# Edge counting in 196 steps, 14 buffered rows, 3125 sources per pass, and one unit's scores made a phase earlier

## The reference

```
x = x + gat8(layernorm(x))       # 8 heads of 32 channels, softmax over each node's incoming edges
x = x + moe(layernorm(x))        # 16 experts, top 2
x = x + gat_3_layers(normalised) # 3 single-head attention layers, 256 channels, gelu between them
x = x + routed_ffn(layernorm(x)) # top half of the tokens through an FFN
```

## Time and profile before

| | us |
|---|---|
| median of three runs | 3741.9 (3736.48 to 3748.98) |
| the profiled execution | 3744.81 |
| its span | 3743.1 |
| edges and nodes (phase 1) | 0 to 66.9 |
| edge counting (phase 2) | 66.9 to 458.1 |
| heads (phase 3) | 458.1 to 1856.5 |
| experts and projection | 1856.5 to 2402 |
| three layers and the last FFN | 2402 to 3743 |

### The profile page before, as it was taken

How to read it: one execution, slowest core, us unless ns; L and a number is a source line. 1 busy time by engine, 2 the same in 40 slices (tenths; PEclk the granted TensorE clock), 3 DMA queues, 4 the chain that set the end, 5 groups by cost and what they waited for, 6 DMA issues and landing times. The chain is left out here.

```text
span 3743.1 us, 70138 instructions
## 1 busy us (share of the span) xinstructions
PE 3425.8 (92%) x27405; PEld 2680.2 (72%) x27406; DVE 2828.5 (76%) x4285; ACT 2523.6 (67%) x4088; POOL 300.4 (8%) x279
## 2 busy tenths in 40 slices
PE   6999889989999898998668999699999999999999
PEld 4565566666666666666458999588878888788777
DVE  7999999999999999999662222665556555676594
ACT  5899899999999999999710111366656665676532
POOL 1000010000000000000003444000000000000000
PEclk9999999999999999999859999899999999999999
DMA  5433211112114121111268885323323232423101
GB/s 163 155 109 140 99 55 65 64 55 73 55 63 202 55 73 55 62 67 55 66 202 267 238 237 150 128 104 106 113 76 119 106 114 75 173 104 121 38 22 35
DMA packets 146630, 398.54 MB, mean 106 GB/s; under 512 B 20163, under 2 KB 92252, under 8 KB 128252
## 3 DMA queue, kind: packets, MB, share of 16 engines
q1 hardware_dynamic: 127542, 354.64, 26.8%
q0 software_dynamic: 15552, 36.16, 4.1%
q10 hardware_dynamic: 3206, 3.20, 0.3%
HBM read 331.96 MB, written 61.99 MB: 105 GB/s over the span
## 5 line engine op out<-in xcount | busy, mean ns | idle before, releaser
L994 PE MATMUL hd_psT<-ident,hd_scores 128*128 128x128 f32 (+1 forms) x5000 | 721.6, 282 | 13.6 <-ACT hd_scores L896 13.6
L905 ACT ACTIVATE hd_probsT<-hd_psT 128x768 f32<-128x768 f32 (+1 forms) x800 | 658.9, 850 | 69.0 <-PE hd_psT L994 69.0
L959 DVE SCALAR_TENSOR_TENSOR hd_scores<-el_heads,hx 128x3136 f32<-128x3136 f32 x200 | 694.9, 3475 | 0.0
L1008 PE MATMUL hd_psO<-hd_probsT,hx 128*32 128x128 f32 (+1 forms) x10000 | 571.3, 281 | 135.1 <-ACT hd_probsT L905 135.1
L963 DVE CUSTOM_DVE_ANT_0 hd_scores<-hd_scores,mask_heads 128x3136 f32<-128x3136 f32 x200 | 684.1, 3421 | 8.6
L896 ACT ACTIVATE hd_scores<-hd_scores,hd_negmax 128x1664 f32<-128x1664 f32 (+1 forms) x400 | 647.9, 1620 | 18.8 <-DVE hd_negmax L963 18.8
L994 PEld LDWEIGHTS hd_psT<-ident,hd_scores 128*128 128x128 f32 (+1 forms) x5000 | 531.8, 140 | 162.7 <-issue 162.7
L1526 PE MATMUL ly_psO<-hx_a,ly_probsT 128*128 128x256 f32 x2500 | 584.0, 381 | 0.0
L1008 PEld LDWEIGHTS hd_psO<-hd_probsT,hx 128*32 128x32 f32 (+1 forms) x10000 | 316.9, 108 | 332.3 <-ACT hd_probsT L905 225.7
L1475 ACT ACTIVATE ly_probsT<-ly_psT 128x768 f32<-128x768 f32 (+1 forms) x300 | 248.4, 828 | 391.8 <-PE ly_psT L1515 391.6
L1526 PEld LDWEIGHTS ly_psO<-hx_a,ly_probsT 128*128 128x128 f32 x2500 | 453.9, 189 | 71.4 <-issue 16.6
(11 more groups left out here) (337 smaller groups left out, 3957.3 us busy)
## 6 DMA issues: line engine op xcount, KB each, us to landing
ly_mask<-mask_dram SPq DMA_DIRECT2D x75, 1568.0 KB, 6.6
mask_heads<-mask_dram SPq DMA_DIRECT2D x48, 1568.0 KB, 6.6
moe_w<-in_L_ffn_w SPq DMA_DIRECT2D x144, 512.0 KB
mask_dram<-logc SPq DMA_DIRECT2D x200, 196.0 KB, 1.9
el_heads<-el_dram POOLq DMA_DIRECT2D x4, 1568.0 KB, 19.3
el_heads<-el_slope_dram POOLq DMA_DIRECT2D x4, 1568.0 KB, 23.0
el_heads<-el_dram SPq DMA_DIRECT2D x4, 1568.0 KB, 10.1
el_heads<-el_slope_dram SPq DMA_DIRECT2D x4, 1568.0 KB, 14.2
```

The lines of the kernel that those rows point to most:

```text
L905: nc.scalar.activation(pT[:, gi % 2, 0:w], psT[gi % 2][:, 0:w], ACT.Copy).then_inc(s_ev, 1)
L959: nc.vector.scalar_tensor_tensor(sc[:, c, :], el[:, h, 0, :], hx[:, b, o:o + 1], el[:, h, 1, :], ALU.subtract, ALU.min).then_inc(s_lk, 1)
L994: last = nc.tensor.transpose(psT[gi % 2][0:r, t * P:(t + 1) * P], sc[:, u % 3, c0:c0 + r], g["ident"][:, :])
L1008: last = nc.tensor.matmul(psO[B % 3][cg * CH:(cg + 1) * CH, h * P:(h + 1) * P], hx[0:r, tt, c0:c0 + CH], pT[0:r, gi % 2, t * P:(t + 1) * P ...
```

## The change

The diff cut to what it does; every use of a score tile in `heads_phase` and `layers_phase` changes from NS to N columns in the same way as those shown.

```diff
-WIN = NP // DL
+WIN = -(-N // DL)
-RUN = 40
+RUN = 28
+LASTROWS = WIN * DL - (NB - 1) * P
...
-def adjacency_phase(nc, g, el, mask):
+def adjacency_phase(nc, g, hx, el, mask, sc_first, nm):
-        SS, AHEAD, ROWS, LATE, OUT = 4, 3, 10, 2, 4
+        SS, AHEAD, ROWS, LATE, OUT = 4, 3, 14, 2, 4
...
-        logc = sb("logc", [P, ROWS, SC])
+        logc = el[:, HG - 1, :, :].rearrange("p i n -> p (i n)")[:, 0:ROWS * SC].rearrange("p (r c) -> p r c", c=SC)
...
             blocks(dve, windows)
+            dve.wait_ge(s_el, 16 * 2 * (HG - 1))
+            dve.wait_ge(s_first, 32)
+            nc.vector.scalar_tensor_tensor(sc_first[:, :], el[:, 0, 0, 0:N], hx[:, 0, D:D + 1], el[:, 0, 1, 0:N],
+                                           ALU.subtract, ALU.min).then_inc(s_lk, 1)
+            dve.wait_ge(s_lk, 1)
+            nc.vector.memset(spare[:, :], 0.0)
+            nc.vector.tensor_tensor_reduce(out=sc_first[:, :], in0=sc_first[:, :], in1=mask[:, 0, 0:N], scale=1.0,
+                                           scalar=3.0e38, op0=ALU.add, op1=ALU.min, accum_out=nm[:, 0:1]).then_inc(s_nm, 1)
+            dve.wait_ge(s_nm, 1)
...
-            for h in range(HG):
+            for h in range(HG - 1):
                 for i, rows in enumerate((g["el_dram"], g["el_slope_dram"])):
                     pool.dma_start(el[:, h, i, :], rows[h:h + 1, 0:NS].broadcast_to([P, NS])).then_inc(s_el, 16)
...
-        sc = sb("scores", [P, 3, NS])
+        sc = [sc_first] + [sb(f"scores{i}", [P, N]) for i in range(1, 3)]
...
         @block.sync
         def _(sp):
+            load_el(sp, 0, HG - 1, 0)
+            load_el(sp, 0, HG - 1, 1)
             for B in range(2, BLOCKS):
...
-                sp.dma_start(mask[:, B % 2, :], g["mask_dram"][b * P:(b + 1) * P, :]).then_inc(s_mask[B % 2], 16)
+                r = P if b < NB - 1 else LASTROWS
+                sp.dma_start(mask[0:r, B % 2, :], g["mask_dram"][b * P:b * P + r, :]).then_inc(s_mask[B % 2], 16)
...
-                if b == 0 and q:
-                    dve.wait_ge(s_el[h], 32 * q)
+                if b == 0 and (q or h == HG - 1):
+                    dve.wait_ge(s_el[h], 32 * (q + (h == HG - 1)))
...
-                nc.vector.scalar_tensor_tensor(sc[:, c, :], el[:, h, 0, :], hx[:, b, o:o + 1], el[:, h, 1, :],
+                nc.vector.scalar_tensor_tensor(sc[c][:, :], el[:, h, 0, 0:N], hx[:, b, o:o + 1], el[:, h, 1, 0:N],
...
-            maxima(0)
+            dve.sem_inc(s_lk, 1)
+            dve.sem_inc(s_nm, 1)
             maxima(1)
...
-        sc = sb("scores", [P, 3, NS])
+        sc = sb("scores", [P, 3, N])
```

More of the change, by code:

```diff
@@ L23 @@
 assert NS >= N and DL * SA == P
-WIN = NP // DL
+WIN = -(-N // DL)
 WPB = P // DL
-RUN = 40
-assert WIN % RUN == 0
+RUN = 28
+assert WIN % RUN == 0 and WIN % 2 == 0
+LASTROWS = WIN * DL - (NB - 1) * P
 ET = -(-E // P)
@@ L85, in edges_nodes_phase @@
         ei = sb("edge_int", [P, 2, EC, P], I32)
-        srcT = sb("srcT", [P, ECOL])
-        dstT = sb("dstT", [P, ECOL])
+        srcT, dstT = (sc_first[:, n:n + ECOL] for n in (0, ECOL))
         tmm = sb("tile_minmax", [P, 2, EC])
@@ L118, in edges_nodes_phase @@
         xT = sb("p0_xT", [P, 2, 2, P])
-        wn = sb("p0_wn", [P, 2, D])
-        wT = sb("p0_wT", [P, 2, D])
+        wn, wT = (sc_first[:, n:n + 2 * D].rearrange("p (k d) -> p k d", k=2) for n in (2 * ECOL, 2 * ECOL + 2 * D))
         A = sb("p0_A", [P, 2, 2 * HEADS])
@@ L801, with heads_phase @@
 CUT = T0[2] * P
-assert sum(TG) * P >= NS > (sum(TG) - 1) * P
+assert sum(TG) * P >= N > (sum(TG) - 1) * P
 @phase
-def heads_phase(nc, g, hx, el, mask, y_dram):
+def heads_phase(nc, g, hx, el, mask, sc_first, nm, y_dram):
     with ExitStack() as ctx:
@@ L962, in maxima @@
                 nc.vector.memset(spare[:, :], 0.0)
-                nc.vector.tensor_tensor_reduce(out=sc[:, c, :], in0=sc[:, c, :], in1=mask[:, B % 2, :],
+                nc.vector.tensor_tensor_reduce(out=sc[c][:, :], in0=sc[c][:, :], in1=mask[:, B % 2, 0:N],
                                                scale=1.0, scalar=3.0e38, op0=ALU.add, op1=ALU.min,
@@ L992, in transposes @@
                     c0 = (T0[gi] + t) * P
-                    r = min(P, NS - c0)
-                    last = nc.tensor.transpose(psT[gi % 2][0:r, t * P:(t + 1) * P], sc[:, u % 3, c0:c0 + r], g["ident"][:, :])
+                    r = min(P, N - c0)
+                    last = nc.tensor.transpose(psT[gi % 2][0:r, t * P:(t + 1) * P], sc[u % 3][:, c0:c0 + r], g["ident"][:, :])
                 last.then_inc(s_T, 1)
@@ L1291, in maxima @@
                 nc.vector.memset(spare[:, :], 0.0)
-                nc.vector.tensor_tensor_reduce(out=sc[:, c, :], in0=sc[:, c, :], in1=mask[:, B % 2, :],
+                nc.vector.tensor_tensor_reduce(out=sc[:, c, :], in0=sc[:, c, :], in1=mask[:, B % 2, 0:N],
                                                scale=1.0, scalar=3.0e38, op0=ALU.add, op1=ALU.min,
@@ L1300, in first_maxima @@
                 c = B % 3
-                cols = (slice(0, EARLY * P), slice(EARLY * P, NS))[part]
+                cols = (slice(0, EARLY * P), slice(EARLY * P, N))[part]
                 if part == 0:
@@ L2186, in program @@
             mask = sbh("mask_heads", [P, 2, NS])
+            sc_first = sbh("scores0", [P, N])
+            nm = sbh("negmax", [P, 3])
             with ExitStack() as early:
```

28 lines of the change are left out of this document (15 added, 13 removed).

## The result

The changed kernel takes 3724.0 us (median of 6 runs, 3716.37 to 3730.57); the kernel before, on the same chip, 3742.2 (6 runs). The ratio is 0.9948, with a 95% interval of 0.9928 to 0.9968: faster by 12 to 27 us, 18.2 by the medians. A second comparison (4 runs against 14) gave 3724.0 against 3739.0: 14.9 us by the medians, ratio 0.9954 (0.9940 to 0.9969). The forecast was 3719.3, between 3710 and 3732, and faster.

A forecast was written before the change was run, and what follows sets the result against it. VectorE was taken to bound the counting and heads phases, TensorE the layers. The terms 7.4 + 5.2 + 5.4 + 4.6 = 22.6 us off the median 3741.9 gave 3719.3 us, range 3710 to 3732.

The forecast's parts named there:

- The bounds: VectorE bounds counting and heads phase, so its savings there come off the end; TensorE bounds the layers, where they don't.
- Four steps: Edge counting: four steps fewer at VectorE's period of 1.857 us save 7.4 us.
- The ring and the loads: Early counting: fourteen rows for ten and six early loads for eight remove ScalarE's waits for stores, saving 5.2 us.
- Unit 0: Crossing from counting to heads: unit 0's score passes fill VectorE's idle time, saving 6.87 less J, 5.4 us.
- J: Cost of VectorE's branch over the looped steps, ahead of unit 0's passes: 0 to 3.3 us, taken as 1.5.
- 3125 columns: Heads phase: eleven columns fewer a pass save 22.9 ns a unit, 4.6 us over 199 units; nothing in the layers.
- The fourth head: Start of heads phase: its late-loaded scores land at 12.3 us, needed at 14.0, so no wait; at worst 1.8 us.
- The crooked buffers: Rival, layers: score buffers off 64-byte boundaries slow TensorE's weight loads, total 3755 to 3897 us; chance 0.05.
- Late loads: Rival, start of heads phase: late fourth head's loads or a long branch, total 3722.9 or 3724.7 us; chance 0.22.
- a ring whose wait moves: Rival, counting: fourteen rows only put the store wait four steps later, total 3724.5 us; chance 0.07.
- ScalarE as the limit: Rival, heads phase: ScalarE becomes the limit and up to 4.6 us of the columns go, 3723.9 us; chance 0.03.

The follow-up runs named there:

- the run without the late clock: The changed kernel with 200 steps for 196, run a second time: counting 387.6 us, total 3723.2 us.
- the reverse experiment: The changed kernel with 3136 columns for 3125 in the heads phase's passes and unit 0's: heads 1391.7 us, total 3727.6 us, ratio 0.9961.

## Why the prediction was right

**The bounds.** VectorE bounds the counting and the heads phase: four steps more, a wait before unit 3, eleven columns more and unit 0 put back each came out at the end of their phase, within 0.5 us of their price once the low clocks are taken off. The layers didn't move with the columns.

**Four steps, 7.4.** Measured 7.8 in the run without the late clock, 7.2 without the 0.6 us at the diagonal.

**The ring and the loads, 5.2.** All of it came: VectorE's steps lost 5.2 us at the waits before, and nothing after. The reason given, slack against the longest landing, held with eight loads too, but its count was wrong. A row is stored nearly three steps after its logarithm and not two, so ten rows leave 13.1 us for 14.9, and fourteen 20.5 for 22.3. The term came out all the same, since 20.5 is over every landing measured (19.5 at most). The same count is why ring 10 with six loads was expected to have no wait, and had one.

**Unit 0, 5.4.** Measured 5.7. The term that was off is J, taken as 1.5 and bounded by 0 and 3.3; it was 1.08. TensorE's row was the right neighbour for the bound and too far for the value. The passes then ended 1.0 us after the last store had landed (447.1 and 446.1), which is what the branch costs, as the step said. The Trainium skill's rule (Runtime: NRT & Kernel Launch, instruction fetch mechanics), that a taken branch out of the held pages waits for a fetch, agrees in sign: with the looped version gone the 1.08 us went. It names no price, and those that the runs show for the same branch, 0.9 to 1.3 us at the end of the counting and 5.5 at its start, are far apart.

**3125 columns, 4.6.** Measured 4.2 by the reverse experiment; 6.85 us a unit.

**The fourth head, 0.** No wait, with a margin of 2.0 us where the rows had given 1.7.

**The rivals.** The crooked buffers didn't show: the weight loads and transposes of the layers are what they were in the earlier trace rows, and the stretch is 340.00 of 340.00.

```profile
L1530 PEld LDWEIGHTS ly_psT<-ident,ly_scores 128*128 128x128 f32 x1719 | 203.1, 142 | 29.0 <-ACT ly_scores L1481 6.9 <-issue 4.6
L1530 PEld LDWEIGHTS ly_psT<-ident,ly_scores 128*53 128x53 f32 x72 | 9.2, 128 | 0.0
...
L1530 PE MATMUL ly_psT<-ident,ly_scores 128*128 128x128 f32 x1719 | 237.5, 275 | 6.6 <-ACT ly_scores L1481 6.6
```

Late loads, a ring whose wait moves and ScalarE as the limit did not show either.

**The total.** The forecast's sum was 22.6, the phases give 22.4, the medians 18.2 with an interval of 12 to 27. The difference of 4.7 us between forecast and median lies inside that interval. The second comparison, 14.9 by the medians with 11.6 to 22.4, ends just short of the sum, so the whole gain may be a few microseconds smaller than the two phases show. What the forecast didn't have is that the phases beside the change vary by more than it allowed: the experts by 16 us over the profiles, and the stretches with a low TensorE clock. Of the twelve profiles of the changed kernel and its variants nine have the 0.6 us at the diagonal, three the 2.0 at the start and four the longest layers (2.6 us over the kernel before); neither of the two profiles of the kernel before and its ring of 8 has any of them. Spread over the twelve that is 0.45 + 0.5 + 0.9, some 2 us. Whether the change makes the low clock likelier isn't settled by two profiles against twelve. That the profiled pair differed by 28.4 us is luck: the two phases gave 22.4 of it.

## What to carry to other kernels

Price a small change phase by phase against the engine that bounds each phase: every term here came within half a microsecond in its phase once the stretches with a low TensorE clock were set aside (up to 2.7 us in the counting), while the totals moved by more than ten between executions. An idle stretch of the bounding engine at a barrier can take work of its own length, if what comes ahead of it, here a branch, is counted. A ring's slack is (rows less the steps until the store is issued) x period; read those steps from a timeline, where the logarithm and the store stand 5.1 us apart here, and compare the slack with the longest landing in the crowded stretch, not with the median.

## What was not expected of the hardware

- The same branch on VectorE costs 1.1 us at the end of the counting and 5.5 us at its start, when broadcast loads have just been issued.
- TensorE's granted clock rose from 0.50 to 1.00 at 76.7 us in one execution and at 82.4 in another of the same kernel, 4.7 and 8.9 us after the phase's first matmul; at the lower clock VectorE waited 1.86 us for it, and the counting lost 2.0 us. After one and the same 2.0 us of idling at the diagonal the clock fell to 0.50 in nine of fourteen profiles and stayed at 1.00 in five, which was worth 0.6 us. Between two layers it stayed low for about 3, 7 or 14 us, and the layers were 1339.6 to 1343.6 us long in the same order.
- The last store of the counting landed 1.9 us after issue without the looped version, and 2.8 to 3.6 us with it in the five profiles read (the kernel before, its ring of 8, the changed kernel, unit 0 back, the scores ahead of the branch). Where VectorE is done first, the next phase waits for it.
- A weight load of 128 x 53 takes 128 ns on average where that of 128 x 64, in the kernel before, took 111. It lay beside other work in both. The group of the kernel before, TensorE's weight loads by shape, 2420 to 3500 us; the one after stands above.

```profile
L1515 PEld LDWEIGHTS ly_psT<-ident,ly_scores 128*64 128x64 f32 x72 | 8.0, 111 | 0.0
```
